# Attention: weights times values once per sequence, other engine orders, masking shared between GpSimd, VectorE and TensorE

## The reference, cut to what matters

```python
# both attention layers, h = layernorm(x); ctx: (32, 375, 256)
q, k, v = heads(h @ w_q), heads(ctx @ w_k), heads(ctx @ w_v)
scores = einsum('bhqd,bhkd->bhqk', q, k) / sqrt(16)
scores = where(mask == 0, -1e9, scores)       # layer 0: one mask, layer 1: one a sequence
attn = softmax(scores, axis=-1)
heads_out = einsum('bhqk,bhkd->bhqd', attn, v)
x = x + tanh(g_xattn[layer]) * (concat(heads_out) @ w_o + b_o)
# after layer 0 a three-matrix feed-forward part, after layer 1 a top-1 mixture of 8 experts
```

## Time and profile before

| | us |
|---|---|
| median of 3 runs | 1952.69 (1951.72 to 1953.31) |
| the profiled execution | 1951.86 |
| its span, first to last instruction | 1949.9 |
| `attention_phase` 0 and 1, first score row to last output sum | 114.9 to 664.6, 1099.2 to 1650.8 |
| one step of the pipeline, in the steady part of both | 16.84 |

### The profile page before, as it was taken

The page is one execution under the profiler, slowest core; times in us unless marked ns, Lnnn a source line. Parts: engine busy times, 40 slices in busy tenths (PEclk is TensorE's granted clock), DMA queues, the critical chain, the costliest instruction groups (busy, mean ns, idle before and its releaser), DMA issues. The chain is left out here.

```text
span 1949.9 us, 40780 instructions
## 1 busy us (share of the span) xinstructions
PE 1614.2 (83%) x15271; PEld 1055.9 (54%) x15271; DVE 1075.8 (55%) x3491; ACT 831.8 (43%) x1822; POOL 859.0 (44%) x842
## 2 busy tenths in 40 slices
PE   1659999999999599999967499999999997706997
PEld 1336666666666355556643256666666664604875
DVE  4646666656666355545536366666666664533653
...
GB/s 203 171 75 80 78 84 86 83 81 83 86 86 66 57 53 56 61 54 57 73 50 170 86 98 102 99 94 92 99 101 99 96 91 27 76 77 152 165 131 26
DMA packets 217955, 175.40 MB, mean 90 GB/s; under 512 B 70058, under 2 KB 211311, under 8 KB 217768
## 3 DMA queue, kind: packets, MB, share of 16 engines
q1 hardware_dynamic: 212136, 163.13, 35.6%
...
...
## 5 line engine op out<-in xcount | busy, mean ns | idle before, releaser
L902 ACT ACTIVATE probs_a<-bank 125x448 f32<-125x448 f32 x768 | 410.6, 538 | 183.5 <-PE bank L782 182.5
L752 PE MATMUL bank<-k_stack_a,q_stack_a 96*128 96x375 f16 x1024 | 315.0, 329 | 72.3 <-DVE row_max_a L952 38.0
L656 POOL TENSOR_TENSOR probs_a<-probs_a,keep_a 125x448 int32<-125x448 int32 x256 | 289.5, 1133 | 147.9 <-ACT probs_a L902 145.8
L656 POOL TENSOR_TENSOR probs_a<-probs_a,mask_keep 125x448 int32<-125x448 int32 x256 | 289.6, 1133 | 146.9 <-ACT probs_a L902 144.7
L952 DVE CUSTOM_DVE_ANT_0 masked_scores_a<-bank,mask_add 112x375 bf16<-112x375 f32 x512 | 269.1, 546 | 148.6 <-PE bank L752 147.0
L952 DVE CUSTOM_DVE_ANT_0 masked_scores_a<-bank,mask_add_a 112x375 bf16<-112x375 f32 x512 | 269.1, 546 | 147.5 <-PE bank L752 144.5
L782 PE MATMUL bank<-q_stack_a,k_stack_a 97*128 97x224 f16 x1536 | 274.1, 260 | 0.1
L664 POOL TENSOR_TENSOR ctx_low_a<-ctx_in_a,ctx_high_a 128x375 f16<-128x375 f32 x128 | 114.8, 898 | 244.3 <-ACT ctx_high_a L875 243.2
L799 PE MATMUL bank<-probs_a,values_a 125*32 125x112 f32 x6144 | 200.4, 263 | 10.4 <-POOL probs_a L656 1.4
L1251 PE MATMUL bank<-h0h_f,ffn_w 128*128 128x448 f16 x512 | 180.6, 353 | 12.0 <-DVE h0l_f L1130 11.9
L799 PEld LDWEIGHTS bank<-probs_a,values_a 125*32 125x32 f32 x6144 | 140.2, 109 | 75.9 <-issue 73.8
...
...
## 6 DMA issues: line engine op xcount, KB each, us to landing
...
k_stack_a<-k_high_a SPq DMA_DIRECT2D x256, 93.8 KB, 3.8
...
k_stack_a<-k_low_a SPq DMA_DIRECT2D x128, 93.8 KB, 3.9
q_stack_a<-q_split SPq DMA_DIRECT2D x128, 84.0 KB, 3.4
...
```

The lines of the kernel that those rows point to most:

```text
L656: pool.tensor_tensor(bits, bits, cols, ALU.mult).then_inc(masked, 1)
L752: pe.matmul(ring(row_use(h))[:, 0:S2], q_stack[x.four][0:STACK, at:at + P], k_stack[x.four][0:STACK, (h // 2) * S2:(h // 2 + 1) * S2], sta ...
L902: act.activation(probs[:, i, :], score_bank[i % 3][0:CK, 0:GT], ACT.Exp, scale=DK ** -0.5).then_inc(exped, 1)
```

## The change

- `weigh` does all 12 units in one block at the end of the sequence's own step. `heads_t` and the next sequence's first exponential wait for the whole block.
- TensorE adds the mask for units 5 and 11 alone. For units 2 and 8 VectorE takes the minimum of the weights and the 0/1 mask times 2^30 (`cut_unit`, a new instruction, twice a step). GpSimd keeps its eight.
- The orders of TensorE, ScalarE, VectorE and GpSimd are written out piece by piece. Score rows 0 and 1 are made a step earlier, for p, near the end of step s; third 2 of the values comes before thirds 0 and 1; the projection moves to the end. GpSimd splits the context after its eight units.
- The ring of row banks is a list (`RING`) from which every wait on a bank is worked out.
- `max_parts` is padded with zeros to 128 columns, so that the transpose of the maxima has 128 columns instead of 8 in its stationary operand.
- The sum of x and bias moves from the attention phase to the queries phase: GpSimd adds the bias to a group of four sequences, SyncE stores it to `x_and_bias` in DRAM. In the attention phase SyncE loads that sum straight into `x_sum`, and waits before it for the store of the sequence two before.
- SyncE sends the key parts half by half: high, high, low of half 0, then of half 1.

```diff
 POOL_UNITS = (0, 1, 3, 4, 6, 7, 9, 10)
+CUT_UNITS = (2, 8)
...
@@ queries_phase, SyncE
-                    wait(sp, xn_ready, s.back(2).value + 1 if s.back(2).exists(NG) else 0)
+                    hold(sp, xn_ready, s.back(2).value + 1 if s.back(2).exists(NG) else 0, passed)
+                    hold(sp, xb_ready, s.back(2).value + 1 if s.back(2).exists(NG) else 0, passed)
                     sp.dma_start(xg[s.slot][:, :, :], take(x_rows, s.value)).then_inc(x_loaded[s.slot], 16)
+                w = s.back(1)
+                if w.exists(NG):
+                    hold(sp, xb_ready, w.value + 1, passed)
+                    sp.dma_start(take(xb_rows, w.value), xb[w.slot][:, :, :]).then_inc(xb_stored[w.slot], 16)
...
+        @block.gpsimd
...
+                    pool.tensor_tensor(xb[s.slot][:, :, :], xg[s.slot][:, :, :],
+                                       m["bo"][layer][:, :].unsqueeze(1).to_broadcast([S, G, D]), ALU.add).then_inc(xb_ready, 1)
...
+HALVES = ("first", "second")
+RING = ((2, 2), (3, "second"), (2, 3), (2, 4), (2, 5), (2, 6), (2, 7), (2, 8), (2, 9), (2, 10), (2, 11), (2, 12),
+        (1, 0), (2, "first"), (2, 13), (2, 14), (1, 1), (2, 15))
...
-        max_parts = sb("max_parts", [S, H], F16)
+        max_parts = sb("max_parts", [S, 2, P], F16)
...
@@ attention_phase, SyncE
-                    wait(sp, based, d.back(2).value + 1 if d.back(2).exists(B) else 0)
-                    sp.dma_start(x_old[d.two][:, :], take(x_in, d.value)).then_inc(x_loaded[d.two], 16)
+                    wait(sp, x_stored[d.two], 16 * d.use2)
+                    sp.dma_start(x_sum[d.two][:, :], take(x_in, d.value)).then_inc(x_loaded[d.two], 16)
...
-                    for g, (tile, ready) in enumerate(((k_high, k_high_ready), (k_low, k_low_ready),
-                                                       (k_high, k_high_ready))):
-                        for n in range(2):
-                            wait(sp, ready, KC * p.value + n + 1)
+                    for n in range(2):
+                        for g, tile, ready in ((0, k_high, k_high_ready), (2, k_high, k_high_ready),
+                                               (1, k_low, k_low_ready)):
+                            sp.wait_ge(ready, KC * p.value + n + 1)
...
@@ GpSimd
-                for i in range(UNITS):
-                    if d.exists(B) and i in pool_units:
+                for i in pool_units:
+                    if d.exists(B):
                         mask_unit(d, i)
-                    if s.exists(B) and i in (2, 8):
-                        low_context(s, i // 8)
-                    if d.exists(B) and i == 5:
-                        base(d)
+                if s.exists(B):
+                    low_context(s, 0)
+                    low_context(s, 1)
...
@@ TensorE: body(s), now (the guards on p, x, d and e left out)
+                units(0)
+                rows(2)
+                    make_keys(p, x, d, e, 0)
+                    turn_maxima(d, 1)
+                rows(3)
+                units(1)
+                rows(4)
+                units(2, 3)
+                rows(5, 6)
+                units(4)
+                    make_keys(p, x, d, e, 1)
+                rows(7, 8)
+                units(5)
+                rows(9)
+                    turn_heads(e)
+                units(6, 7)
+                    make_values(x, p, e, (2,))
+                rows(10)
+                units(8)
+                    turn_heads_back(e)
+                units(9)
+                rows(11)
+                    make_values(x, p, e, (0, 1))
+                rows(12)
+                units(10)
+                    score_row(p, 0)
+                    turn_maxima(x, 0)
+                units(11)
+                rows(13)
+                    project(e, x)
+                rows(14)
+                    score_row(p, 1)
+                rows(15)
+                    weigh(d)
...
@@ ScalarE: body(s), now: heads_t(e), exp 0, high_keys(p, 0), maxima(d, 1), exp 1 to 4,
@@   split_context(s, 0), high_keys(p, 1), split_context(s, 1), exp 5 to 7, values(x, third 2),
@@   exp 8, heads_n(e), exp 9, values(x, thirds 0 and 1), exp 10, maxima(x, 0), exp 11
...
@@ VectorE
+            def cut_unit(d, i):
...
+                dve.scalar_tensor_tensor(out=weights, in0=cols, scalar=MASKED, in1=weights, op0=ALU.mult,
+                                         op1=ALU.min).then_inc(cut, 1)
...
+                rows(2, 3)
+                    low_keys(p, 0)
+                rows(4, 5)
+                    cut_unit(d, CUT_UNITS[0])
+                rows(6, 7)
+                    low_keys(p, 1)
+                    normalise(e)
+                    shift_parts(x, 0)
+                rows(8, 9, 10, 11)
+                    cut_unit(d, CUT_UNITS[1])
+                rows(12)
+                    reduce_row(p, 0)
+                rows(13)
+                    add_output(e)
+                rows(14)
+                    reduce_row(p, 1)
+                rows(15)
+                    shift_parts(x, 1)
```

294 lines of the change are left out of this document (155 added, 139 removed).

## The result

The changed kernel takes 1959.73 us (median of 20 runs, 1950.06 to 1979.75), the kernel before beside it 1951.44: a ratio of 1.004, interval 1.0028 to 1.0053. It is slower by 0.4%, where 1837 us had been predicted, and 1959.73 lies outside the range of 1775 to 1893. The profiled execution took 1957.49 us, 5.6 more than that of before.

A forecast was written before the change was run, and what follows sets the result against it. TensorE's in-order work was taken to bound each 16.84 us step; 28 steps at 14.7 and 28 at 15.1 save 60 and 49, ramps 8, queries phases cost 2: 115 off 1951.86 gives 1837 us, range 1775 to 1893.

The forecast's parts named there:

- The step without the new wait: Attention step: 16.84 us less mask, block, maxima and old-wait savings, plus 0.25 for one remaining wait, gives 13.85 us.
- The new wait: TensorE at row 0 of p, waiting for the last key part: 0.85 us a step in layer 0, 1.25 in layer 1.
- The masks of layer 1: SyncE's two extra mask transfers and a higher DMA share lengthen layer 1's key wait from 0.85 to 1.25 us.
- Queries phases: GpSimd's bias addition and SyncE's stores there: +1 us a phase, bounds 0 and +4, two phases +2.
- third rival: VectorE minima and GpSimd block each other in attention, step 15.8 us on the mean: 1888 us, chance 0.17.
- Maxima: TensorE's two transposes of the maxima, padded to full width: -0.35 us a step, bounds 0 and -0.4.
- Masks: Two TensorE mask matmuls of 0.20 us go: -0.40 us a step, with VectorE's two minima hidden.
- The first: Rival: no waits left in attention, the step is TensorE's own 13.85 us or less: 1770 us, chance 0.16.
- the second rival: SyncE becomes a loop of its own through store, loads and keys, 16.6 and 17.4 us a step: 1969 us, chance 0.05.
- The fourth rival: The attention layout misses waits and half the saving comes back, 16 us a step: 1905 us, chance 0.12.
- The step predicted at 14.7 and 15.1: Full attention step with the new wait included: 14.7 us in layer 0, 15.1 in layer 1, instead of 16.84.
- the gain of 8 us at the ramps: Four more steps a layer that have units but lack a stage: 1 us gained each, 8 in all.

The follow-up runs named there:

- rows_back: The changed kernel with score rows 0 and 1 of p put back into their own step, the ring of banks adapted: 1850.37 us, ratio 0.9491.
- filler: The changed kernel with nine extra matmuls, which change no result, ahead of row 0 of p: 1954.17 us, ratio 1.0011.
- thin_masks: rows_back with layer 1's mask transfers cut to 32 columns and 4 partitions from the fifth sequence on: 1789.46 us, ratio 0.916.
- loads_late: rows_back with the full loads of x and the masks issued behind the six key parts: 1787.31 us, ratio 0.916.
- best: loads_late with the old bias path, but GpSimd adding the bias of the sequence four before at the start of its step: 1767.54 us, ratio 0.9069.
- pad_only: The kernel before with only the maxima padded to 128 stationary columns for their transpose: 1929.91 us, ratio 0.9895.
- cut_only: The kernel before with only the mask part: VectorE minima behind rows 5 and 12, two mask matmuls fewer: 1984.55 us, ratio 1.0183.
- bias_back: rows_back with the old bias path, GpSimd adding the bias in the attention step behind unit 4: 2078.01 us, ratio 1.0643.

## Why the prediction was wrong, step by step

- **The step without the new wait, 13.85 us: the sum came out.** rows_back has 13.82 in layer 0, and in the changed kernel's own step 15.97 - 2.27 = 13.70. The block (2.4 predicted, 2.44), row 0 due at 9.1 us (9.07), the last key part issued 6.1 to 6.6 us after unit 0 (6.18), and the waits for row banks (9.5 us in 24 steps) came as laid out. Some luck is in it. The pieces listed behind row 0 add to 4.5 us where 4.7 was written (4.63 in the step above), and of the terms of the sum only the maxima's was measured alone.
- **The new wait, 0.85 us with ends 0 and 2.1: the step that failed.** It priced the last key part with the median landing of a part, 3.8 us of the earlier trace rows. The row waits for the last of six. They are issued 0.6 us apart and land 0.98 us apart, so the last takes 5.1 us: it lands 11.28 us after unit 0, not at 9.9 to 10.4. The number was there to be read: in the kernel before, the train took 8.2 us from its first issue (300.93) to its last landing (309.1), after the change 8.3 (306.35 to 314.66). I had the time of one instruction where I needed that of a queue. The change issues them closer together, and the last took 5.1 us where it had taken 4.3. In layer 0 the wait was 1.8 us a step, twice the 0.85.
- **What hangs on the wait was left out.** In the changed kernel TensorE's granted clock falls to half 7 times in the steady part of layer 0 and 13 times in layer 1, 75 us together; before it did so nowhere in the steady part of attention. filler shows about 0.5 us a step for it in layer 0, which is the rest of that layer's miss of 1.4 a step.
- **The masks of layer 1, +0.4: too little by 2 us, and at the wrong place.** I put their traffic on the keys, and the keys' wait came as forecast there (1.2 us a step against 1.25). It delays the small maxima transfer for unit 6, which I gave no wait at all: 37 us in the changed kernel, and after rows_back 2.1 us a step (15.92 against 13.82), which thin_masks and loads_late both take away. The change issues x behind a store's landing, 1.1 us later than SyncE could (301.84 to 302.94). The prediction counted this in SyncE's own time (maxima out near 2.3, first key part at 3.0; they came at 2.2 and 3.0), but not that it brings x, masks, queries, maxima and keys closer together.
- **Queries phases, +2: +18.** The addition takes 2.36 us as estimated (2.3), and it is not what the next load waits for. In both phases each load but the first two starts 0.1 to 0.4 us after a normalisation on VectorE has ended. That normalisation goes from SBUF to SBUF, and beside the addition it takes 3.3 to 3.4 us instead of 1.38: in four of the eight groups of the first phase, 8 us of its 10, but in only one of the second phase. It is the third rival's mechanism, at a place where the prediction did not put it. TensorE's clock also fell to half for 3.4 or 6.8 us twice in the first phase and once in the second, at points where before it was full; how the rest, most of the 8.3 us of the second phase above all, divides is not shown. loads_late to best, which takes the addition out of these phases, brings 20 us back.
- **Maxima, -0.35: -0.39 alone** (pad_only), 22 us against the 21 expected.
- **Masks, -0.40: not to be had alone.** In the old order +0.39 a step (cut_only). That the matmuls' 0.40 is inside the 13.82 of the new order, where VectorE has slack, is argued from the sum and was not measured apart.
- **The third rival, the minima beside GpSimd: the mechanism is real, and the minima's price in the changed kernel is small.** Most minima take 0.72 or 0.95 us and wait for the multiplication under way, as the prediction's bound had it; GpSimd's multiplication rises from 1133 to 1231 ns. But the bound of one multiplication was no bound: 5.4 us in bias_back. And rows of the kernel before do show such a wait (the negation above, 2.64 us instead of 0.16), though the prediction found none. The Trainium skill, page "SBUF — State Buffer", section "Who interferes with whom", gives the lock for a whole instruction. The 0.72 to 0.95 us agree with it; in bias_back the wait went on over five instructions.
- **The first and the second rival did not happen.** SyncE is no loop of its own: the store lands in 1.9 us. Rival two's outcome, slower, came by two other ways. The fourth rival, a layout that misses waits, was the nearest: it put the step at 16, and the steps were 16.12 and 17.10.

The step predicted at 14.7 and 15.1 was 16.12 and 17.10: 40 + 56 us of the miss. The queries phases are 16, and the other 8 of the 121 (1957.49 - 1837) are the gain of 8 us at the ramps that the sum had counted and that did not come.
